# A three-layer decoder block: mended boundaries between batches, and loops written out as straight code

## The chip, the cores and the metric

The kernel runs on one core of one Trainium2 chip. The metric is the device time of one execution in microseconds; lower is better. Before the change it was 4486.38 us in the median of three runs (4477.06, 4486.38 and 4491.97).

## What is computed

The input is `x` (batch B = 4, sequence S = 1024, width D = 512), a context of the same shape, and a mask of 4 × 1024 × 1024. Three layers follow each other, each closed by a residual sum and a layer norm. Both attentions have 16 heads of 32.

```python
# layer 1, "att 0": gated self-attention
aperture, expression = sigmoid(x @ Wa + ba), sigmoid(x @ We + be)
inner, outer = heads(x @ Wi), heads(x @ Wo)
attn = softmax(inner @ outer.T / sqrt(dh)) * aperture[..., :, None] * expression[..., None, :]
attn = attn / (attn.sum(-1) + 1e-8)
x = layernorm(x + rotate_per_head(attn @ heads(x @ Wv)) @ Wout)
# layer 2, "att 1": masked cross-attention
scores = where(mask == 0, -1e9, (x @ Wq.T + bq) @ (ctx @ Wk.T + bk).T / sqrt(dk))
x = layernorm(x + (softmax(scores) @ (ctx @ Wv.T + bv)) @ Wo.T + bo)
# layer 3: 16 experts, weights rw of each token, causal attention of width 64
q, k, v = (sum_e rw_e * (x @ proj[e]) for proj in (q_proj, k_proj, v_proj))
attn = softmax(where(causal, q @ k.T / 8, -inf)) @ v
x = layernorm(x + sum_e (rw_e * attn) @ o_proj[e])
```

## The kernel before, in words

**Attention.** Both attention layers are one program, `attention`. A batch of a layer is worked in eight *pairs* of heads; a pair goes over eight key tiles of 128. TensorE (PE) makes the scores of a tile ("st", L955, and in layer 2 the mask of keys, L958), ScalarE (ACT) takes their exponentials from a PSUM bank (L1159), PE multiplies by V ("pv", L889). Beside that run the row maxima of a later pair: "sm" on PE (L906), the reduction on VectorE (DVE; L1396 in layer 1, L1392 with the mask of queries in layer 2). When 16 maxima of a pair are there, "mneg" puts them into one row: PE L914, ACT L1102, and a DMA from ACT's queue (L1106) into the tile `stack`, from which "st" reads. SyncE (SP) fills the rest of `stack` by DMAs ("stack", L614); `stack` 0 and 1 hold the first two pairs.

Between two batches stands a *boundary*: V of the next batch ("V", eight tiles, L847, evicted by DVE at L1354); the normalisation of the last pair ("norm", seven parts in layer 2: L1417, L1421 and L1427); the output projection of the old batch ("ct", "out": ACT L1083, GpSimd (POOL) L827, PE L847, DVE L1450 to L1460, in layer 2 after POOL has added the bias to the residual, "bo", L820); layer norm ("root", ACT L1166, "ln", DVE L1257); K and Q of the next batch ("K", "Q", L847), where the group 0 of each is split in two parts by ACT (L1056) and DVE (L1307); a transposed copy of the result ("xt", PE L1014, ACT L1172), stored by ACT's queue as two transfers of 1 MB into `x_t` (L1179); the result itself stored by SP as one of 2 MB ("store", L632); and in layer 2 the column means of V ("CS", PE L1000, DVE L1402 to L1408) and 16 tiles of mask converted by DVE ("mask", L1347), of which eight are done in the last pair and eight in the boundary. Then pair 0 of the next batch starts with its first "st".

`section_steps(att, nxt)` writes all of this as one list of steps for the stretch "pairs of layer `att`, then the boundary to a batch of layer `nxt`". Every engine runs down this list and issues the steps that are its own, in the list's order. `with_maxima` interleaves the 16 first "sm" with the projections. PSUM is shared as a ring of two half banks (V, K, Q, out, st, xt, CS) and of two wide ones (sm, mneg), filled in the list's order.

The lists are used as five plans. Each engine runs them as

```python
run(Section(plans[0]))                  # opening, to the first batch
with pe.Fori(0, B - 1) as i:
    run(Section(plans[1], i))           # layer 1 to layer 1, three times
run(Section(plans[2]))                  # layer 1 to layer 2
with pe.Fori(0, B - 1) as i:
    run(Section(plans[3], i))           # layer 2 to layer 2, three times
run(Section(plans[4]))                  # the end of layer 2
```

The branches that close PE's two loops stand at L1020 and L1023. Within a loop a semaphore is waited for at a value that grows with `i`: it stands in a register, which an instruction (`REGISTER_ALU`) computes first. Between such waits `alone(eng)` puts an extra instruction that counts up a semaphore which nobody waits for. So that each pass uses whole rounds of a ring, a pass ends with an extra unit where a count is odd ("wpad", L927, and "xpad", L1016).

**Experts.** `expert_layer` does 32 tiles of 128 tokens with eight banks: "p" (PE L1785 with `w_in_e`, DVE multiplies by the weights, POOL adds), "turn", "score", "pv", "out" (PE L1785 with `w_out_e`) and routing on DVE. `token_slot(g, tile)` is the order of one slot, in which the tiles g−1 and g−2 are finished beside tile g. An opening of two slots, a loop of three passes with eight slots each (PE's branch: L1853) and a closing of eight slots follow each other.

Of the kernel before, what the change touches and what calls it, by code (L numbers as in the profile page):

```python
# [6 lines left out]
P = 128  # L7
# [27 lines left out]
HALF_KINDS = ("Q", "K", "EX", "AP", "V", "CS", "st", "out", "xt", "xpad")  # L35
WIDE_KINDS = ("sm", "mneg", "sel", "RZ", "wpad")
# [77 lines left out]
def mask_places(att):  # L114

    if att == 1:
        return {("K", n // 2): (TT + n, 2) for n in range(0, TT, 2)}
# [6 lines left out]
def section_steps(att, nxt):  # L124
# [67 lines left out]
    if nxt is not None:  # L192
# [3 lines left out]
        if nxt == 1:  # L196
# [4 lines left out]
            ks[len(more) - 1] += [("load", "xq", 0), ("load", "xq", 1), ("mxload", 0), ("mxload", 1)] + store  # L201
# [3 lines left out]
            steps += [("Q", 0, 0)] + xt[:2] + [("Q", 0, 1), ("stack", 0), ("Q", 1, 0), ("Q", 1, 1)] + xt[2:HALF]  # L205
            steps += with_maxima([("Q", g, c) for g in (2, 3) for c in range(NC_)], (4, 3, 3, 3))
            steps += first + [("CS", n) for n in range(4)] + xt[HALF:HALF + 2]
            steps += [("mneg", 0), ("stack", 1)] + xt[HALF + 2:]
        else:
# [3 lines left out]
            ks[len(more) - 1] += store  # L213
            ks[5].append(("stack", 0))
# [5 lines left out]
            steps += first + xt[:HALF] + [("mneg", 0), ("stack", 1)] + xt[HALF:]  # L220
# [14 lines left out]
class Plan:  # L235

    def __init__(self, number, att, nxt, loop, steps):

        self.number, self.att, self.nxt, self.loop, self.steps = number, att, nxt, loop, steps


class Section:

    def __init__(self, plan, i=None):

        self.number, self.att, self.nxt, self.loop, self.steps = plan.number, plan.att, plan.nxt, plan.loop, plan.steps
        self.i = i
        one = lambda b: bass.ds(b, 1)
        self.batch = one(i if plan.loop else B - 1)
        self.next_batch = one(i + 1 if plan.loop else 0)  # L250


class Count:
# [13 lines left out]
    def before(self, sec):  # L267

        return self.after(sec, 0)
# [1945 lines left out]
```

## Time and profile before

| | |
|---|---|
| median of three runs | 4486.38 us (4477.06 to 4491.97) |
| the profiled execution | 4494.6 us, its span 4492.8 us |
| PE busy | 4115.9 us (92%) |
| DVE busy | 2571.8 us (57%) |
| ACT busy | 1714.3 us (38%) |
| POOL busy | 1774.8 us (40%) |
| granted TensorE clock, mean | 0.961 |

The span reaches from the first to the last instruction of the profiled execution, whose own time is 1.8 us more. In the rows below a line of the timeline reads: start in us, busy us, engine, code line, operation, output<-input, shapes, the number of instructions merged in it, and in brackets the idle time before it and what ended that. PEld is the weight load of PE; a name with q (ACTq, PEldq) is the sequencer of the engine.

### The profile page before, as it was taken

The numbers are of one execution on the slowest core, as the hardware profiler recorded it, in microseconds if no ns is written. First come the engines' busy times: TensorE is split into PE (matmuls) and PEld (weight loads), VectorE is DVE, ScalarE is ACT, GpSimd is POOL, SyncE is SP. The second block draws the span as 40 slices with busy tenths as digits, with TensorE's granted clock in tenths as the row PEclk, the third lists the DMA queues.
The fourth block names the chain that finished last, engine by engine and source line by source line (L and its number), as shares of the span: only waits on it lengthen the run. The fifth ranks groups of instructions, "written<-read, shape, count | busy, mean of one in ns | idle before, by whom it ended". The sixth has DMA issues, their size and how long they took to land. (4 is left out here: it accounts for less than half of the span.)

```text
span 4492.8 us, 65435 instructions
## 1 busy us (share of the span) xinstructions
PE 4115.9 (92%) x20596; PEld 2370.4 (53%) x20596; DVE 2571.8 (57%) x4094; ACT 1714.3 (38%) x3120; POOL 1774.8 (40%) x1251
## 2 busy tenths in 40 slices
PE   7999899989999998999799989997998599999998
PEld 5344643554364436444544464446443477777776
DVE  4563466346445646674667466756674556565564
ACT  2554255335524552443244324442444322222222
POOL 0323121312222133675367535753663243444443
PEclk9999899989999999999999989998999799999998
DMA  3321322142123224222422242223220300000000
GB/s 96 76 69 42 104 50 53 51 109 50 50 71 86 56 81 137 65 56 91 119 56 57 90 113 62 52 95 108 66 43 20 139 24 27 30 29 30 29 29 12
DMA packets 136379, 294.73 MB, mean 66 GB/s; under 512 B 19856, under 2 KB 37904, under 8 KB 136016
## 3 DMA queue, kind: packets, MB, share of 16 engines
q1 hardware_dynamic: 125520, 272.93, 22.5%
q10 hardware_dynamic: 10496, 17.31, 1.1%
q8 instruction: 185, 3.03, 0.3%
q14 instruction: 178, 1.46, 0.1%
HBM read 145.74 MB, written 43.25 MB: 42 GB/s over the span
## 5 line engine op out<-in xcount | busy, mean ns | idle before, releaser
L1159 ACT ACTIVATE probs_a<-half_a 128x512 f32<-128x512 f32 x2048 | 1123.8, 595 | 992.5 <-PE half_a L958 464.4
L955 PE MATMUL half_a<-stack_a 97*128 97x512 f32 x2048 | 873.3, 485 | 79.6 <-ACT probs_a L1159 48.4
L1396 DVE TENSOR_REDUCE mx_a<-wide_a 128x1 f32<-128x1024 f32 x512 | 604.5, 1220 | 535.6 <-PE wide_a L906 529.9
L1392 DVE CUSTOM_DVE_ANT_0 wide_a<-wide_a,mask_q_a 128x1024 f32<-128x1024 f32 x512 | 619.8, 1245 | 286.6 <-PE wide_a L906 273.2
L906 PE MATMUL wide_a<-stack_a 96*128 96x512 f32 x2048 | 676.1, 435 | 52.1 <-DVE mx_a L1392 19.8
L955 PEld LDWEIGHTS half_a<-stack_a 97*128 97x128 f32 x2048 | 377.8, 194 | 623.4 <-ACT probs_a L1159 356.1
L795 POOL TENSOR_TENSOR psums_a<-psums_a,probs_a 128x1024 f32<-128x1024 f32 x232 | 557.5, 2423 | 140.0 <-ACT probs_a L1159 115.3
L1785 PE MATMUL work_e<-w_in_e,x_e 128*128 128x512 f32 x2304 | 574.2, 401 | 18.5 <-DVEq L2041 11.2
L889 PE MATMUL acc_a<-probs_a,v_a 128*32 128x512 f32 x4096 | 555.0, 613 | 3.1 <-ACT u_a L1130 3.0
L906 PEld LDWEIGHTS wide_a<-stack_a 96*128 96x128 f32 x2048 | 377.7, 194 | 233.2 <-issue 64.3
L1785 PEld LDWEIGHTS work_e<-w_in_e,x_e 128*128 128x128 f32 x2304 | 430.0, 191 | 120.5 <-issue 20.3
L958 PE MATMUL half_a<-mask_k_a,eye_a 128*128 128x512 fp8e5 x1024 | 407.9, 398 | 0.0
L1753 POOL TENSOR_TENSOR weighted_e<-weighted_e 128x512 f32<-128x512 f32 (+2 forms) x288 | 242.1, 841 | 189.1 <-DVEq L2068 150.6
L889 PE MATMUL acc_a<-probs_a,e_one_a 128*2 128x512 f32 x2048 | 269.9, 599 | 0.0
L759 POOL MEMSET stack_a<- 1x2048 f32 x16 | 28.8, 1799 | 520.0 <-PE half_a L847 519.0
L958 PEld LDWEIGHTS half_a<-mask_k_a,eye_a 128*128 128x128 fp8e5 x1024 | 100.8, 98 | 233.3 <-issue 211.1
L847 PE MATMUL half_a<-stack_a,wkv_a 128*128 128x512 f32 x768 | 190.0, 406 | 34.7 <-DVE first_a L1307 28.5
L847 PE MATMUL half_a<-w_a,ct_a 128*128 128x512 f32 x768 | 187.5, 401 | 25.9 <-POOLq L828 19.8
L847 PE MATMUL half_a<-stack_a,w_a 128*128 128x512 f32 x768 | 204.2, 411 | 3.2 <-DVEq L1325 2.2
L2063 DVE TENSOR_TENSOR weighted_e<-work_e,rw_e 128x512 f32<-128x512 f32 x192 | 132.8, 692 | 111.3 <-PE work_e L1785 65.6
L1785 PE MATMUL work_e<-w_out_e,mixed_t_e 128*128 128x512 f32 x768 | 186.4, 399 | 3.3 <-DVEq L2113 3.3
L847 PEld LDWEIGHTS half_a<-stack_a,wkv_a 128*128 128x128 f32 x768 | 150.7, 197 | 71.6 <-DVE first_a L1307 30.2
(244 smaller groups left out, 4586.7 us busy)
## 6 DMA issues: line engine op xcount, KB each, us to landing
stack_a<-qk_a SPq DMA_DIRECT2D x336, 256.0 KB, 4.9
y_a<-x SPq DMA_DIRECT2D x8, 2048.0 KB, 8.9
x<-y_a SPq DMA_DIRECT2D x8, 2048.0 KB, 8.5
mstage_a<-mask SPq DMA_DIRECT2D x32, 512.0 KB, 4.1
mstage_a<-mask_t SPq DMA_DIRECT2D x32, 512.0 KB, 4.2
stack_a<-first_a SPq DMA_DIRECT2D x48, 256.0 KB, 4.7
stage_a<-x_t SPq DMA_DIRECT2D x20, 512.0 KB, 3.7
x_t<-xts_late_a ACTq DMA_DIRECT2D x10, 1024.0 KB, 8.0
```

What stands on the lines that cost most here:

```text
L795: op = lambda h: pool.tensor_tensor(psums[:, h, :], psums[:, h, :], probs[:, kt % 2 * 2 + h, :], ALU.add)
L847: last = pe.matmul(out, a(k), b(k), start=(k == 0 and n == 0), stop=(k == KT - 1 and n == 2))
L889: last = pe.matmul(out, left, right[:, c * CH:(c + 1) * CH], start=opens or ((kt == 0) and not (masked and part)), stop=closes or ((kt == ...
L906: last = pe.matmul(bank[:, c * CH:(c + 1) * CH], stack[0:3 * DH, SLOT[p], h, t * P:(t + 1) * P], stack[0:3 * DH, SLOT[p], 2 + h, c * CH:(c ...
L955: last = pe.matmul(bank[:, :], stack[0:3 * DH + 1, s, 2 + h, kt * P:(kt + 1) * P], stack[0:3 * DH + 1, s, h, c * CH:(c + 1) * CH], start=T ...
L958: last = pe.matmul(bank[:, :], eye8[:, :], mask_k[:, kt, c * CH:(c + 1) * CH], start=False, stop=True)
L1159: act.activation(probs[:, kt % 2 * 2 + h, c * CH:(c + 1) * CH], bank[:, :], ACT.Exp, scale=SCALE).then_inc(free, 1)
L1392: dve.tensor_tensor_reduce(bank[:, :], bank[:, :], mask_q[:, t, :], 1.0, -3e38, ALU.add, ALU.max, mx[:, p % 3, n:n + 1]).then_inc(free, 1)
L1396: dve.tensor_reduce(mx[:, p % 3, n:n + 1], bank[:, :], AX.X, ALU.max).then_inc(free, 1)
L1753: pool.tensor_tensor(buf[:, 0:n], buf[:, 0:n], buf[:, n:2 * n], ALU.add)
L1785: last = pe.matmul(out, a(k), b(k), start=(k == 0 and n == 0), stop=(k == tiles - 1 and n == 2))
L2063: dve.tensor_tensor(prod.rearrange("p (e d) -> p e d", d=HD), bank[:, :].rearrange("p (e d) -> p e d", d=HD), rw[:, t, (w % 2) * 8:(w % 2) ...
```

## The change

The change has two halves.

**Mended boundaries.** In the list of steps:

- Layer 2 to layer 2: the masks 8 to 14 move from the first four K steps, two at each, to V1 to V7, one at each, and mask 15 goes behind out 0. The parts of the last pair's "norm" stand one at a V tile (before, two at V1, V2 and V3).
- In all boundaries "store" comes behind "stack 0" (before, ahead of it).
- Boundary to layer 2: Q(0,0), Q(0,1), stack 0, store, then xt 0 to 3, then Q of the groups 1, 2 and 3 with all 16 "sm" among them, then xt 4 and 5, mneg 0, stack 1, xt 6 and 7, and one "CS" with all 16 small matmuls in one bank and one eviction. Before, xt 0 and 1 stood between the two Q(0), Q of group 1 ahead of the first "sm", three "sm" behind the last Q, and four "CS" units ahead of xt 4.
- Boundary to layer 1: three xt, then mneg 0, stack 1 and five xt (before, four and four). On ACT's queue the row of mneg 0 so goes out ahead of the first `x_t` store.
- ACT runs a one-element exponential (`warm`) behind the second square root of each boundary, and behind the sine of the opening.

**No loops.** Attention has ten plans, one for each batch of each layer and the two ends, and the experts one list of 32 tiles. Every wait is for a constant. The registers, `alone` and the units "wpad", "xpad" and "pad" are gone.

```diff
 def mask_places(att):
     if att == 1:
-        return {("K", n // 2): (TT + n, 2) for n in range(0, TT, 2)}
+        return {**{("V", n + 1): (TT + n, 1) for n in range(TT - 1)}, ("out", 0): (2 * TT - 1, 1)}
...
         for n in range(1 if att == 0 else 7):
-            tail[(n + 1) // 2 + (1 if att == 0 else 0)].append(("norm", PAIRS - 1, n))
+            tail[n + (1 if att == 0 else 0)].append(("norm", PAIRS - 1, n))
...
-            ks[len(more) - 1] += [("load", "xq", 0), ("load", "xq", 1), ("mxload", 0), ("mxload", 1)] + store
+            ks[len(more) - 1] += [("load", "xq", 0), ("load", "xq", 1), ("mxload", 0), ("mxload", 1)]
             for step in ks[:-2]:
                 steps += step
             steps += [("xs", 0, k) for k in range(KT)] + ks[-2] + ks[-1] + [("xs", 1, k) for k in range(KT)]
-            steps += [("Q", 0, 0)] + xt[:2] + [("Q", 0, 1), ("stack", 0), ("Q", 1, 0), ("Q", 1, 1)] + xt[2:HALF]
-            steps += with_maxima([("Q", g, c) for g in (2, 3) for c in range(NC_)], (4, 3, 3, 3))
-            steps += first + [("CS", n) for n in range(4)] + xt[HALF:HALF + 2]
-            steps += [("mneg", 0), ("stack", 1)] + xt[HALF + 2:]
+            steps += [("Q", 0, 0), ("Q", 0, 1), ("stack", 0)] + store + xt[:HALF]
+            steps += with_maxima([("Q", g, c) for g in (1, 2, 3) for c in range(NC_)], (2, 3, 3, 3, 3, 2))
+            steps += xt[HALF:HALF + 2] + [("mneg", 0), ("stack", 1)] + xt[HALF + 2:] + [("CS",)]
         else:
...
-            ks[len(more) - 1] += store
-            ks[5].append(("stack", 0))
+            ks[5] += [("stack", 0)] + store
...
-            steps += first + xt[:HALF] + [("mneg", 0), ("stack", 1)] + xt[HALF:]
+            steps += xt[:HALF - 1] + [("mneg", 0), ("stack", 1)] + xt[HALF - 1:]
...
-    if att == nxt:
-        for kinds, name in ((WIDE_KINDS, "wpad"), (HALF_KINDS, "xpad")):
-            if sum(s[0] in kinds for s in steps) % 2:
-                steps.append((name,))
...
-    plans = [Plan(number, att, nxt, loop, section_steps(att, nxt)) for number, (att, nxt, loop) in enumerate(
-        ((None, 0, False), (0, 0, True), (0, 1, False), (1, 1, True), (1, None, False)))]
+    layers = (None,) + (0,) * B + (1,) * B + (None,)
+    plans = [Plan(n, att, nxt, (n - 1) % B, section_steps(att, nxt)) for n, (att, nxt) in enumerate(zip(layers, layers[1:]))]
...
-        def alone(eng):
-
-            eng.sem_inc(apart, 1)
...
                     elif step in (("out", HALF), ("root",)):
                         c = int(kind == "root")
...
-                        alone(act)
                         act.activation(sd[:, half], tmp[:, half], ACT.Sqrt).then_inc(sd_ready, 1)
+                        if c:
+                            act.activation(warm[:, :], eye[:, 0:1], ACT.Exp)
...
-            run(Section(plans[0]))
-            with act.Fori(0, B - 1) as i:
-                run(Section(plans[1], i))
...
+            for plan in plans:
+                run(plan)
```

**How the instructions move, at three places.** The first is DVE in the boundary from layer 2 to layer 2, where K is split: `first_a` is the part of K that the next matmuls on `stack_a` wait for, `mask_k_a` a mask tile, `w_a` a weight chunk. Before:

```order
L1304 ISA
L1307 SCALAR_TENSOR_TENSOR first_a<-half_a,bk_a,first_a 128x512
L1340 REGISTER_ALU
L1347 TENSOR_SCALAR mask_k_a<-mstage_a 128x1024 x2
L1332 REGISTER_ALU
L1334 TENSOR_TENSOR w_a<-stage_a,w_a 128x1024
L1340 REGISTER_ALU
L1347 TENSOR_SCALAR mask_k_a<-mstage_a 128x1024 x2
L1332 REGISTER_ALU
L1334 TENSOR_TENSOR w_a<-stage_a,w_a 128x1024
L1340 REGISTER_ALU
L1347 TENSOR_SCALAR mask_k_a<-mstage_a 128x1024 x2
```

and now:

```order
L1196 SCALAR_TENSOR_TENSOR first_a<-half_a,bk_a,first_a 128x512
L1221 TENSOR_TENSOR w_a<-stage_a,w_a 128x1024 x2
L1134 RECIPROCAL rstd_a<-sd_a 128x4
L1136 TENSOR_TENSOR sd_a<-rstd_a 128x4
L1138 TENSOR_TENSOR sd_a<-sd_a,tmp_a 128x4
L1140 TENSOR_SCALAR sd_a<-sd_a 128x4
L1142 TENSOR_TENSOR rstd_a<-rstd_a,sd_a 128x4
L1148 TENSOR_SCALAR y_a<-y_a,mv_a,rstd_a 128x512 x2
L1196 SCALAR_TENSOR_TENSOR first_a<-half_a,bk_a,first_a 128x512
```

The eight mask tiles no longer stand between the two `first_a`. They now stand in the V phase of the same boundary, between the evictions `v_a`:

```order
L1239 TENSOR_TENSOR v_a<-half_a,bv_a 128x512
L1232 TENSOR_SCALAR mask_k_a<-mstage_a 128x1024
L1299 RECIPROCAL u_a<-u_a 128x128
L1239 TENSOR_TENSOR v_a<-half_a,bv_a 128x512
L1232 TENSOR_SCALAR mask_k_a<-mstage_a 128x1024
L1299 RECIPROCAL u_a<-u_a 128x128
L1239 TENSOR_TENSOR v_a<-half_a,bv_a 128x512
```

where before there was an eviction, then two parts of the norm at some tiles and none at others.

The second place is PE at the end of the same boundary, from the last "sm" (`wide_a<-stack_a`) to the first "st" (`half_a<-stack_a`). Before:

```order
L906 MATMUL wide_a<-stack_a 128x512 x2
L997 REGISTER_ALU
L1000 MATMUL half_a<-ones_a,vsum_a 32x1 x4
L943 REGISTER_ALU
L1000 MATMUL half_a<-ones_a,vsum_a 32x1 x8
L943 REGISTER_ALU
L1000 MATMUL half_a<-ones_a,vsum_a 32x1 x4
L1014 MATMUL half_a<-eye_a,y_a 128x128 x4
L943 REGISTER_ALU
L1014 MATMUL half_a<-eye_a,y_a 128x128 x4
L912 REGISTER_ALU
L914 MATMUL wide_a<-neg_eye_a,mm_a 16x128
```

and now:

```order
L837 MATMUL wide_a<-stack_a 128x512 x2
L778 MATMUL half_a<-stack_a,w_a 128x512 x6
L944 MATMUL half_a<-eye_a,y_a 128x128 x8
L845 MATMUL wide_a<-neg_eye_a,mm_a 16x128
L944 MATMUL half_a<-eye_a,y_a 128x128 x8
L930 MATMUL half_a<-ones_a,vsum_a 32x1 x16
L886 MATMUL half_a<-stack_a 128x512
```

A Q unit stands behind the last "sm", the CS matmuls behind everything, and the pad unit and the branch are gone.

The third is ACT at the end of a boundary from layer 1 to layer 1 (`mrow_a` is the row of maxima, `xts_early_a` the first half of the transposed copy). Before:

```order
L1172 ACTIVATE xts_early_a<-half_a 128x4x128 x2
L1177 ISA
L1179 ISA
L1179 DMA x_t<-xts_early_a 128x4x512
L503 REGISTER_ALU
L1102 ACTIVATE mrow_a<-wide_a 16x128
L1104 REGISTER_ALU
L1106 DMA stack_a<-mrow_a 1x16x128
```

and now:

```order
L1070 ACTIVATE xts_early_a<-half_a 128x4x128 x3
L1016 ACTIVATE mrow_a<-wide_a 16x128
L1019 DMA stack_a<-mrow_a 1x16x128
L1070 ACTIVATE xts_early_a<-half_a 128x4x128
L1076 DMA x_t<-xts_early_a 128x4x512
```

The row is copied and sent before the first `x_t` store instead of behind it.

## Rows read from the trace of the kernel before

**Rows 1.** The page: the span, and the DMA queue "instruction" (packets, MB, share).
```profile
span 4492.8 us, 65435 instructions
...
q8 instruction: 185, 3.03, 0.3%
```

**Rows 2.** Windows, two boundaries: from:to, length, busy PE, PEld, DVE, ACT, POOL, then clock.
```profile
418.00:540.00 122.00, 108.28 (x473) 86.12 (x466) 54.05 (x78) 24.67 (x40) 27.54 (x20) 0.94 0.33 96
...
3011.00:3150.00 139.00, 115.63 (x497) 89.12 (x489) 83.56 (x129) 29.15 (x47) 50.40 (x33) 0.89 0.39 114
```

**Rows 3.** Groups by line: busy us, mean ns | idle us before, releaser.
```profile
L1159 ACT ACT_TABLE_LOAD x8 | 10.3, 1283 | 44.0 <-issue 24.3 <-PE half_a L955 17.4 <-PE half_a L958 2.3
```

**Rows 4.** Timeline, mneg 0 to the first "st": in the opening, then after an untaken branch.
```profile
113.05 0.38 PE L914 MATMUL wide_a<-neg_eye_a,mx_a 128*16 128x128 f32 x2
...
117.68 0.51 PE L955 MATMUL half_a<-stack_a 97*128 97x512 f32 x1 [4.25 <-DMA stack_a<-mrow_a]
...
1370.06 0.39 PE L914 MATMUL wide_a<-neg_eye_a,mx_a 128*16 128x128 f32 x2
...
1371.17 0.41 ACTq L1179 DMA_DIRECT2D x_t<-xts_early_a  x1
...
1379.43 1.19 PE L955 MATMUL half_a<-stack_a 97*128 97x512 f32 x2 [3.18 <-DMA stack_a<-mrow_a]
```

**Rows 5.** Timeline, first boundary between batches of layer 1: "store", and the first "sm".
```profile
482.75 0.39 SPq L632 DMA_DIRECT2D x<-y_a  x1
...
493.97 2.08 PE L906 MATMUL wide_a<-stack_a 96*128 96x512 f32 x4 [3.11 <-DMA stack_a<-qk_a]
```

**Rows 6.** Timeline of the last boundary of layer 2 to layer 2, around K and Q.
```profile
3088.50 0.69 DVE L1347 TENSOR_SCALAR mask_k_a<-mstage_a 128x1024 fp8e5<-128x1024 int32 x1 [2.55 <-DMA mstage_a<-mask_t]
...
3089.91 7.84 PE L847 MATMUL half_a<-stack_a,wkv_a 128*128 128x512 f32 x24 [9.06 <-DVE first_a L1307]
...
3104.11 0.66 PE L1014 MATMUL half_a<-eye_a,y_a 128*128 128x128 f32 x4 [2.45 <-DVE first_a L1307]
...
3109.64 4.94 PE L847 MATMUL half_a<-stack_a,w_a 128*128 128x512 f32 x21
...
3116.67 1.21 PE L906 MATMUL wide_a<-stack_a 96*128 96x512 f32 x4 [0.66 <-DMA stack_a<-first_a]
```

**Rows 7.** Instructions of DVE that write `mask_k`: ns least/median/most, first and last start.
```profile
L1347 DVE TENSOR_SCALAR mask_k_a<-mstage_a x32: 679/695/1782, 1697.5 to 3088.5; 128x1024 fp8e5<-128x1024 int32 x32
```

**Rows 8.** PE's branches (ns least/median/most), and the first "st" behind a taken one.
```profile
L1020 PEldq COMPARE_BRANCH  x3: 83/5658/7010, 532.3 to 1375.5; - x3
...
L1023 PEldq COMPARE_BRANCH  x3: 83/4589/4834, 2241.2 to 3147.3; - x3
...
L1853 PEldq COMPARE_BRANCH  x3: 79/4164/4281, 3823.0 to 4281.7; - x3
...
539.57 1.22 PE L955 MATMUL half_a<-stack_a 97*128 97x512 f32 x2 [6.67 <-issue]
```

**Rows 9.** Timeline, row DMAs of layer 1: a batch in the loop, the batch behind it.
```profile
577.70 0.58 ACTq L1106 DMA_DIRECT2D stack_a<-mrow_a  x1
...
724.35 0.51 ACTq L1106 DMA_DIRECT2D stack_a<-mrow_a  x1
...
1417.09 0.54 ACTq L1106 DMA_DIRECT2D stack_a<-mrow_a  x1
...
1562.13 0.53 ACTq L1106 DMA_DIRECT2D stack_a<-mrow_a  x1
```

**Rows 10.** Timeline, "out" of the same tiles: around a taken branch, in the closing.
```profile
4029.43 0.94 PE L1785 MATMUL work_e<-w_out_e,mixed_t_e 128*128 128x512 f32 x3
...
4199.54 0.70 PE L1785 MATMUL work_e<-w_out_e,mixed_t_e 128*128 128x512 f32 x2
...
4258.79 0.94 PE L1785 MATMUL work_e<-w_out_e,mixed_t_e 128*128 128x512 f32 x3
...
4422.35 0.94 PE L1785 MATMUL work_e<-w_out_e,mixed_t_e 128*128 128x512 f32 x3
```

More of the change, by code:

```diff
@@ L281, in __init__ @@
         self.count = Count(plans, lambda plan, s: s[0] in kinds)
-        assert not any(n % size for n, plan in zip(self.count.length, plans) if plan.loop)
     def place(self, sec, step):
-        c, size = self.count, self.size
-        n = c.base[sec.number] + c.at[sec.number][step]
-        return n % size, sec.i * (c.length[sec.number] // size) + n // size if sec.loop else n // size
+        n = self.count.upto(sec, step) - 1
+        return n % self.size, n // self.size
     def opens(self, sec, step):
-        return not sec.loop and self.place(sec, step)[1] == 0
+        return self.place(sec, step)[1] == 0
 WAITING = {}
@@ L313, in attention @@
     loads = kind_count("load")
+    assert not any(len(some) % 2 for some in loads.at)
     pool_splits = Count(plans, lambda plan, s: s[0] == "vsum" or (s[0] == "split" and not fast(plan, s[1])))
@@ L318, in attention @@
     los = Count(plans, two_engine)
-    assert not any(n % 2 for n in loads.length)
     stacks = [Count(plans, lambda plan, s, k=k: s[0] == "stack" and SLOT[s[1]] == k) for k in range(SLOTS)]
@@ L1193, in run @@
                         act.drain().then_inc(turn_sem, 1)
[L1195 to L1201 removed]
+                        act.activation(warm[:, :], eye[:, 0:1], ACT.Exp)
+            for plan in plans:
+                run(plan)
         @block.vector
@@ L1735, in _, with run @@
             pool.sem_inc(stored, 1)
-            def run(sec):
-                for step in sec.steps:
+            def run(steps):
+                for step in steps:
                     kind = step[0]
@@ L1787, in parts, with run @@
                 return last
-            def run(sec):
-                for step in sec.steps:
+            def run(steps):
+                for step in steps:
                     kind = step[0]
@@ L1847, in run @@
                                      lambda k: w_out[:, 0, k, :], lambda k: w_out[:, 1, k, :], FK)
-                    else:
-                        last = pe.matmul(bank[:, 0:P], ones[:, :], eye[:, :], start=True, stop=True)
                     last.then_inc(work_full[b], 1)
-            run(Section(plans[0]))
-            with pe.Fori(0, B - 1) as i:
-                run(Section(plans[1], i))
-            run(Section(plans[2]))
+            run(plan.steps)
         @block.scalar
@@ L1863, in _, with run @@
             act.drain().then_inc(norm_sem, 1)
-            def run(sec):
-                for step in sec.steps:
+            def run(steps):
+                for step in steps:
                     kind = step[0]
@@ L2030, in route, with run @@
                 dve.drain()
-            def run(sec):
-                for step in sec.steps:
+            def run(steps):
+                for step in steps:
                     kind = step[0]
@@ L2138, in run @@
                         dve.drain().then_inc(rstd_ready, 1)
[L2140 to L2143 removed]
+            run(plan.steps)
 def constants():
```

369 lines of the change are left out of this document (91 added, 278 removed).

## The prediction

> **What bounds the kernel now.** I read first the page's busy times: PE works 92% of the span, so only what PE waits for, or what it does at the lower clock, can be won. The page also gives the instruction stream, 65435 instructions in 4492.8 us [rows 1]. Then the windows, to find where PE is idle. Inside the pairs it is nearly full; the idle time stands in the boundaries. In one of layer 1, PE is busy 108.28 of 122.00 us at a granted clock of 0.94, in one of layer 2 115.63 of 139.00 us at 0.89 [rows 2]. PE runs at one of two clocks (1.2 or 2.4 GHz), so a mean of 0.94 over 122 us is 2 × 0.06 × 122 = 14.6 us at half speed, a loss of 7.3 us; in layer 2 it is 30.6 us and a loss of 15.3. Then the timelines of the boundaries, for what ended each wait [rows 4 to 6], and last the branches and the pace of equal stretches with and without registers [rows 8 to 10].
>
> **Table load.** The first exponential of each batch has a table load of 1.28 us ahead of it, eight in all [rows 3]. It starts when the first scores are there, and both half banks stay full until it ends, so PE waits with it. `warm` puts it behind the second square root, where ACT has slack beside the layer norm of DVE. I count all of it: 8 × 1.28 = 10.3 us. If it delays an eviction of K there, part comes back; if all of it did, the term is 0.
>
> **Three boundaries of layer 1.** (a) The 2 MB store is issued at 482.75, ahead of `stack` 0, and the first "sm" waits 3.11 us for that [rows 5]. With `stack` 0 ahead of the store I take all of it, and 1.5 us of the 7.3 that the clock costs there, since the clock falls behind this wait: 4.6 each. Nobody waits for the store before the first exponential of the next batch, so a later store costs nothing. (b) From mneg 0 to the first "st" it is 1379.43 − 1370.06 = 9.37 us, since the row's DMA is issued behind the 1 MB `x_t` store of 1371.17. In the opening, where no such store exists, it is 117.68 − 113.05 = 4.63 us [rows 4]. The difference is 4.7; five xt stand there now instead of four, about 0.7 us more, which I subtract: 4.0 each. The xt units fill PE in the meantime, so they cost nothing until the row lands; the evictions of five on ACT (about 3 us) fit in the 4.6. (c) Behind a taken branch the first "st" comes after 6.67 us of idle time [rows 8], behind the untaken one after 3.18 [rows 4]: 3.5 us more, twice. Sum: 3 × 8.6 + 7 = 32.8 us.
>
> **Boundary from layer 1 to layer 2.** No branch and no masks moved. It takes the new order of Q, xt, stack and store, bounded by 0 and the sum of (a) above and (b) below, 4.6 + 3.8 = 8.4 us; I take 5.
>
> **Three boundaries of layer 2.** (a) K of group 1 waits 9.06 us for DVE's `first_a`, which stands behind masks that themselves wait for their DMA (2.55 us before the last one). The 24 matmuls behind that wait take 7.84 us where the later ones take 4.94/21 × 24 = 5.65: 2.2 us at the lower clock. With the masks out of the K steps both go: 11.3 us [rows 6]. (b) From there to the first "sm" Q and xt alternate: 2.45 us of waiting at 3104.11, then 0.66 before "sm" at 3116.67, with only xt and Q of group 1 as cover. With the two Q(0) back to back `stack` 0 is issued about one eviction and one xt pair earlier. This is between 2.45 us (that wait alone) and 5.8 (both waits, and the four xt at 0.66 each that stood in the chain); I take 3.8, nearer to the waits that a row shows. Four CS units, each waiting for its eviction, become one off the path: 0.6. (c) Seven masks now stand between the evictions of V. DVE's own time for one is 0.70 us in the median but 1.78 at most [rows 7]. V gives DVE a tile in 12 × 4.94/21 = 2.8 us [rows 6], so seven add between 0 (they fit in the gaps) and 7 × 0.70 = 4.9; nearer to the gaps, since "ct" waits for POOL's bias sums anyway: +1.5. (d) The two taken branches cost 4.59 and 4.83 us [rows 8], 9.4 in sum, of which some of the fetch lies beside the wait for the row: 8. Sum: 3 × (11.3 + 3.8 + 0.6 − 1.5) + 8 = 50.6 us.
>
> **Pairs.** Between the same two row DMAs, four pairs apart, a batch in the loop takes 724.35 − 577.70 = 146.65 us, the batch behind it, with constant waits, 1562.13 − 1417.09 = 145.04: 0.40 us a pair [rows 9]. 24 pairs of layer 1 give 9.7 us. For layer 2 I show no such pair of rows; bounds are 0 and 9.7, I take the middle, 4.8. `alone` goes in all 64: 0 to 5, I take 2.5. Sum: 17 us.
>
> **Experts.** Six slots around the last taken branch take 4199.54 − 4029.43 = 170.1 us, the same six in the closing 4422.35 − 4258.79 = 163.6 [rows 10]. Of the 6.5 us the branch is 4.2 [rows 8] and registers the other 2.3, or 0.39 a slot. 24 slots give 9.4, two branches 8.4, pads and `alone` about 3: 21 us.
>
> **The sum** is 10.3 + 32.8 + 5 + 50.6 + 17 + 21 = 136.7 us, against the profiled execution's 4494.6: 4357.9. That execution is 8.2 above the median, 4486.4, so I predict **4350 us**.
>
> **What a taken branch costs.** PE's own record shows it: 7.01 and 5.66 us in layer 1, 4.83 and 4.59 in layer 2, 4.28 and 4.16 in the experts; untaken 0.08 [rows 8]. The Trainium skill ("Advanced Engine Details and Errata", section Control Flow Timing) gives a compare-and-branch as about 108 ns. By that figure six would cost 0.65 us together, the 23.4 us that my sum has for them would be 0.6, and the time 4373. The trace disagrees for taken ones, and decides.
>
> **Rivals.**
>
> *The waits come back elsewhere.* In layer 2, V becomes bound by DVE: eight masks of 0.70 at V are 5.6 us, the first "sm" waits for `stack` as it does in layer 1, 3.1 us, and the clock falls behind that wait, 2.2 us; three times, 32.7. And `warm` only moves its 10.3 us. For it: in the boundary of layer 2 DVE is the second busiest, 83.56 of 139 us [rows 2], and single masks took 1.78 us, over twice the median [rows 7], so something on the chip can slow them. Against it: PE had 23 us of idle time in that window, which is room. The time is 4350 + 43 = 4393. The Trainium skill ("SBUF — State Buffer", section Who interferes with whom) says that VectorE and GpSimd share one pair of ports under an exclusive lock. No row here shows the lock itself, and the sentence before goes by the masks' times alone. Chance 0.20.
>
> *Only the loops count.* The boundaries are bound by work that I take for cover, and the new order gives nothing: what is left is the branches (23.4), pairs (17) and experts without their branches (12.6), 53 us: 4433. For it: the boundary's matmuls are the same. Against it: waits of 9.06 and 3.11 us with nothing else that PE could do. Chance 0.07.
>
> *The clock stays up.* The half-speed losses of six boundaries are 3 × 7.3 + 3 × 15.3 = 68 us [rows 2], of which my sum has only 11. If shorter waits keep PE at the full clock for some 60% of the rest, 34 us come on top, and 10 more if the pairs of layer 2 and `alone` reach their upper bounds: 4306. Chance 0.14.
>
> *Straight code stalls.* Here the kernel gets slower. The code of three passes now stands in memory three times, PE alone has nearly twice as many instructions, and each must be brought in once. Its place is every block of code that arrives late; its price is what a taken branch costs, which is such an arrival with nothing fetched ahead: 4.2 us at least [rows 8]. 33 of these eat the 137 us; from 36 on the kernel is slower by over 0.3%, and with 60 it stands at 4486 − 137 + 250 = 4600. Against it: a loop's passes are fetched again each time, so the 3.03 MB of the instruction queue [rows 1] hardly change, and the stretches without a loop run faster than those within, not slower [rows 9, 10]. Chance 0.02. The Trainium skill ("Runtime: NRT & Kernel Launch", section Instruction fetch mechanics) says that a taken branch outside the window forces a fetch while straight code is fetched ahead, its cost mostly hidden. The trace agrees with both halves.
>
> **Chances and range.** My forecast has 0.57, the rivals 0.20, 0.07, 0.14 and 0.02. A measurement of this kernel can tell about 0.3%, 13 us, from no change. Four of the five cases, 0.98, lie further below than that; 0.02 of these I move to "the same", for faults that no case names, so faster 0.96, same 0.02, slower 0.02. The range reaches from just under the clock case to 12 us above the case of the waits that come back: 4300 to 4405. Above it lie the two last-named bad cases (0.09) and little else; below it the better half of the clock case. The unknown terms alone (0 to 10.3 for the table, 0 to 7.8, three times 0 to 4.9, 0 to 9.7, 0 to 5) move the forecast by less than 30 us either way.
>
> **What would show it.** In the changed profile: no table load between the first "st" and the first exponential; from mneg 0 to the first "st" about 5 us in layer 1, where 9.4 stood; no wait of PE for `first_a` above 1 us in K of layer 2, and a clock of 0.92 or more in that window; no wait of the first "sm" above 1 us; a boundary from the last "pv" to the first of some 118 us in layer 1 and 133 in layer 2; expert slots of equal length in all four batches. I am wrong if V of layer 2 spreads by over 5 us, if "sm" waits 3 us for `stack`, or if PE has gaps of 4 us and more with nothing to release them, away from any boundary.

## The result and the profile after

The changed kernel takes 4324.1 us (4323.7 to 4327.5, four runs), the kernel before beside it 4483.1: a ratio of 0.9644, 95% interval 0.9632 to 0.9655. That is 159 us or 3.6% faster. I had forecast 4350 and a range of 4300 to 4405; the gain is 22 us larger than the forecast's 137. But the experiments show that its two halves are not the ones I had summed up. In the two profiled executions, from which the rows and the table by stage come, the difference is 4492.8 − 4322.0 = 170.8 us, since the one of the kernel before lies above its median.

The page of the changed kernel, as [rows 1]:

```profile
span 4322.0 us, 56842 instructions
...
q8 instruction: 165, 2.70, 0.3%
q14 instruction: 112, 0.92, 0.1%
```

8,600 instructions fewer are executed, and fewer packets of code are fetched than before, though the program is longer: 165 + 112 packets, where the page before has 185 [rows 1] and, on its second queue,

```profile
q14 instruction: 178, 1.46, 0.1%
```

The windows of the same two boundaries as [rows 2], now from the last "pv" to the first of the next batch (after the clock stand the mean share of the DMA engines that was busy, and GB/s):

```profile
409.50:521.30 111.80, 108.45 (x482) 85.54 (x474) 55.54 (x80) 29.37 (x49) 26.03 (x18) 0.99 0.34 98
2893.00:3026.00 133.00, 115.01 (x514) 88.26 (x506) 88.69 (x127) 33.77 (x56) 51.58 (x33) 0.94 0.43 129
```

The windows of [rows 2] leave out the last 8 and 10 us of their boundaries. The whole ones before:

```profile
418.10:548.20 130.10, 113.98 (x484) 89.20 (x476) 55.61 (x80) 29.49 (x48) 32.75 (x22) 0.91 0.32 92
3011.40:3159.80 148.40, 123.25 (x512) 93.00 (x505) 85.52 (x132) 34.28 (x55) 50.52 (x33) 0.87 0.43 122
```

In layer 1 PE idled 16.1 of 130.1 us at a granted clock of 0.91, and now idles 3.4 of 111.8 at 0.99; in layer 2 it idled 25.2 of 148.4 at 0.87, and now 18.0 of 133.0 at 0.94.

Table loads by line, as [rows 3]: L1062 is the square root, which had its eight loads before as well, and L1064 is `warm`. No exponential of attention has one any more.

```profile
L1062 ACT ACT_TABLE_LOAD x8 | 10.3, 1283 | 0.1
L1064 ACT ACT_TABLE_LOAD x8 | 10.3, 1283 | 0.1
```

Timeline, end of the first boundary of layer 1, as [rows 4], and its stack 0 and store, as [rows 5]:

```profile
510.21 0.39 PE L845 MATMUL wide_a<-neg_eye_a,mx_a 128*16 128x128 f32 x2
...
511.17 0.53 ACTq L1019 DMA_DIRECT2D stack_a<-mrow_a  x1
...
512.45 0.59 ACTq L1076 DMA_DIRECT2D x_t<-xts_early_a  x1
...
515.32 0.76 PE L886 MATMUL half_a<-stack_a 97*128 97x512 f32 x2 [0.43 <-DMA stack_a<-mrow_a]
...
474.90 5.92 SPq L582 DMA_DIRECT2D stack_a<-qk_a  x6
...
480.87 1.27 SPq L597 DMA_DIRECT2D x<-y_a  x1
```

The row goes out ahead of the `x_t` store, and the first "st" starts 5.1 us after mneg 0, where it was 9.37. PE waits 0.43 us there. The store (480.87) comes behind stack 0 (474.90).

Timeline of K, Q and the first "sm" in the last boundary of layer 2, as [rows 6]:

```profile
2950.16 19.41 PE L778 MATMUL half_a<-stack_a,wkv_a 128*128 128x512 f32 x84 [0.34 <-DVE y_a L1329]
...
2978.76 1.09 PE L944 MATMUL half_a<-eye_a,y_a 128*128 128x128 f32 x8 [1.19 <-DVE first_a L1196]
...
2985.24 1.19 PE L837 MATMUL wide_a<-stack_a 96*128 96x512 f32 x2 [4.47 <-DMA stack_a<-first_a]
```

K runs through without the wait of 9.06 us, but the first "sm" now waits 4.47 us for `stack` 0, where it waited 0.66.

The conversions of the mask, as [rows 7], now beside V:

```profile
L1232 DVE TENSOR_SCALAR mask_k_a<-mstage_a x32: 681/1055/2287, 1629.2 to 2925.1; 128x1024 fp8e5<-128x1024 int32 x32
```

Their median rose from 0.70 to 1.06 us and the longest from 1.78 to 2.29. In both kernels those that ran while POOL did nothing took 0.69 us, and those above 0.75 us all ran beside an instruction of POOL; in V that is above all the bias sum of "bo". V itself did not become longer by it: its 96 matmuls take 22.1 us in these boundaries before and after.

Pace of four pairs, as [rows 9], and of six expert slots, as [rows 10]:

```profile
549.38 0.53 ACTq L1019 DMA_DIRECT2D stack_a<-mrow_a  x1
...
693.93 0.53 ACTq L1019 DMA_DIRECT2D stack_a<-mrow_a  x1
```

```profile
3876.39 0.70 PE L1621 MATMUL work_e<-w_out_e,mixed_t_e 128*128 128x512 f32 x2
...
4036.69 0.70 PE L1621 MATMUL work_e<-w_out_e,mixed_t_e 128*128 128x512 f32 x2
```

144.55 us, where 146.65 (loop) and 145.04 (behind it) stood, and 160.3 us, where 170.1 and 163.6 stood. So both are shorter than the stretches that already had constant waits.

A table by stage, from the starts of the first and last "pv" of each batch and of the first and last unit "out" of the experts (us in the profiled executions; the last three columns are experiments told below):

| stage | before | after | e1_straight_old | e2_alone | p1_cs_early |
|---|---|---|---|---|---|
| opening | 126.1 | 122.2 | 123.9 | 124.1 | 122.5 |
| pairs of layer 1, four batches | 1158.6 | 1143.8 | 1143.2 | 1152.3 | 1145.3 |
| three boundaries of layer 1 | 386.6 | 337.6 | 366.0 | 339.9 | 336.1 |
| boundary 1 to 2 | 138.4 | 132.5 | 130.8 | 136.7 | 127.5 |
| pairs of layer 2 | 1194.9 | 1188.9 | 1181.3 | 1196.7 | 1181.3 |
| three boundaries of layer 2 | 452.0 | 398.4 | 417.6 | 412.5 | 385.8 |
| to the first expert "out" | 145.2 | 142.3 | 142.3 | 147.6 | 143.7 |
| experts | 875.0 | 839.9 | 839.5 | 863.7 | 839.9 |
| rest | 15.9 | 16.5 | 16.7 | 15.9 | 16.6 |

Four fifths of the 170.8 us come from three places: 49 us in boundaries of layer 1, 54 in those of layer 2, 35 in the experts.

### The profile page after: what moved, and what is told of

It reads as the page before. It is cut to its first block and busy times, and to the rows that moved or that the text cites. A ratio compares the mean times of both kernels' runs of the same rounds, so it can differ in the third digit from the quotient of the medians.

```text
span 4322.0 us, 56842 instructions
## 1 busy us (share of the span) xinstructions
PE 4054.9 (94%) x20584; PEld 2348.4 (54%) x20584; DVE 2600.2 (60%) x4082; ACT 1718.5 (40%) x3131; POOL 1788.5 (41%) x1251
## 5 line engine op out<-in xcount | busy, mean ns | idle before, releaser
L886 PE MATMUL half_a<-stack_a 97*128 97x512 f32 x2048 | 862.8, 480 | 42.9 <-ACT probs_a L1056 24.0
L837 PE MATMUL wide_a<-stack_a 96*128 96x512 f32 x2048 | 671.1, 432 | 44.1 <-DMA stack_a<-first_a 18.1
L778 PE MATMUL half_a<-stack_a,wkv_a 128*128 128x512 f32 x768 | 179.4, 391 | 6.5 <-DVE y_a L1329 5.2
L778 PEld LDWEIGHTS half_a<-w_a,ct_a 128*128 128x128 f32 x768 | 146.9, 193 | 67.7 <-issue 21.8
```

The costliest lines, as they stand in the source:

```text
L778: last = pe.matmul(out, a(k), b(k), start=(k == 0 and n == 0), stop=(k == KT - 1 and n == 2))
L837: last = pe.matmul(bank[:, c * CH:(c + 1) * CH], stack[0:3 * DH, SLOT[p], h, t * P:(t + 1) * P], stack[0:3 * DH, SLOT[p], 2 + h, c * CH:(c ...
L886: last = pe.matmul(bank[:, :], stack[0:3 * DH + 1, s, 2 + h, kt * P:(kt + 1) * P], stack[0:3 * DH + 1, s, h, c * CH:(c + 1) * CH], start=T ...
```

## The experiments

Each run is compared with the kernel before on the same chip; the median of before lay between 4483 and 4489 in these comparisons. Differences against the changed kernel are therefore taken from the ratios (0.001 is 4.5 us); each ratio is uncertain by 0.0012 to 0.0020, which makes a difference of two uncertain by 8 to 10 us. A stage of the table rests on one execution of each kernel.

### Which half does it: e1_straight_old

Straight code with constant waits, every boundary as before.

```diff
-            steps += [("Q", 0, 0), ("Q", 0, 1), ("stack", 0)] + store + xt[:HALF]
+            steps += [("Q", 0, 0)] + xt[:2] + [("Q", 0, 1), ("stack", 0), ("Q", 1, 0), ("Q", 1, 1)] + xt[2:HALF]
...
-            steps += xt[:HALF - 1] + [("mneg", 0), ("stack", 1)] + xt[HALF - 1:]
+            steps += first + xt[:HALF] + [("mneg", 0), ("stack", 1)] + xt[HALF:]
```

and so on for all lines of `section_steps` and `mask_places`, CS and `warm`.

> The changed kernel without loops, registers, alone and pads, but with every boundary as before (masks in K, store ahead of stack 0, xt and Q in the old order, four CS, no warm). Against 4483 before and 4324 after. Theory 1 (the two halves add up, each about as large as my terms say, experts and pairs larger): branches 23, pairs 21, experts without branches 27: 4412 (4400 to 4425), experts as short as in the changed kernel. Theory 2 (the loops carry nearly all, boundaries were mostly longer for the registers in them): 4350 to 4370. Theory 3 (boundaries carry nearly all): 4440 or more.

Measured: 4362.6 us, ratio 0.9721 (0.9708 to 0.9735). 125 us of the 160 come with the loops alone, 35 with the boundaries. That is theory 2, whose 4350 to 4370 it hits; my own sum had 53 for the loops (branches 23.4, pairs 17, experts without branches 12.6) and 84 for the boundaries and the table load. The windows of the same two boundaries:

```profile
411.40:533.40 122.00, 111.42 (x482) 87.36 (x474) 55.58 (x80) 29.25 (x48) 30.54 (x22) 0.95 0.32 96
2929.40:3067.80 138.40, 116.35 (x514) 88.32 (x507) 88.17 (x132) 34.14 (x55) 50.64 (x33) 0.93 0.44 131
```

By the table, a boundary of layer 1 falls from 129 to 122 us without its order being touched, one of layer 2 from 151 to 139. In the profiled executions the loops are worth 131.5 us: 63 in the seven boundaries, 29 in the pairs, 35.5 in the experts, the rest at the ends.

### What in the loops: e2_alone, e9_alone_pe, e10_alone_act

```diff
+        def alone(eng):
+            eng.sem_inc(apart, 1)
```

called again where it was called before: e2 on all engines, e9 on PE, e10 on ACT.

> The changed kernel with alone(eng) back at all of its 100-odd places in the code. My sum gives alone 5.5 us in all: 4330. Rival: the experts won 35 us where I forecast 21, and the 14 more are the extra instructions between waits, on ACT and PE at every unit of a bank: 4340 to 4350, with the experts 14 us longer than in the changed kernel and the pairs within 5 us.

> The changed kernel with alone back on PE only (5 places in the code). With all of them the kernel took 65 us more. Theory 1 (the extra instruction delays the engine that is the bound, so PE's own are half of it or more): 4356 or more. Theory 2 (it lengthens the chains by which PE gets its banks back, so they sit on ACT and DVE): 4335 or less here.

> The changed kernel with alone back on ACT only (36 places in the code). Theory 1 (PE's own count): 4324 to 4335. Theory 2 (chains over ACT: in the run with all of them PE waited 9.7 and 9.6 us more in the experts for ACT's steps behind turn and prob_t): 4344 to 4365.

Measured: e2 4389.3, ratio 0.9778 (0.9765 to 0.9792), so 60 us for an instruction that does nothing, more than either expectation had. e9 4323.4, ratio 0.9639 (0.9619 to 0.9658): no difference. e10 4347.2, ratio 0.9689 (0.9671 to 0.9706): 20 us. If the parts add, the rest, some 40 us, is on DVE, POOL and SP together; it was not split further. How many there are and how long each lasts (ns least/median/most), of attention (L474) and experts (L1597) in e2:

```profile
L474 DVEq EVENT_SEMAPHORE  x940: 21/21/21, 16.3 to 3406.6; - x188
L474 ACTq EVENT_SEMAPHORE  x729: 17/17/38, 13.8 to 3414.3; - x183
...
L1597 DVEq EVENT_SEMAPHORE  x560: 21/21/50, 3445.0 to 4383.6; - x187
L1597 PEldq EVENT_SEMAPHORE  x537: 51/51/51, 3475.2 to 4370.1; - x179
L1597 ACTq EVENT_SEMAPHORE  x430: 17/17/17, 3436.6 to 4383.2; - x144
```

PE has 541 of 51 ns and pays nothing that a measurement can tell. But not every `alone` is one instruction more: the pages of the changed kernel, e2, e9 and e10 begin

```profile
span 4322.0 us, 56842 instructions
span 4389.5 us, 60013 instructions
span 4323.9 us, 57093 instructions
span 4340.6 us, 57602 instructions
```

All 4,444 of e2 add 3,171 instructions, PE's 541 add 251 and ACT's 1159 add 760; the others stand where the changed kernel has some other semaphore instruction. 251 of 51 ns are 12.8 us of PE's sequencer, and 760 of 17 ns are 12.9 us of ACT's. The first cost nothing, the second 20 us (10 to 30 with the uncertainty), so the length alone doesn't give the price. That ACT's come between PE and a bank that it waits for is the reading that theory 2 had, and its total came true; its place did not: only 4 of e10's 18.6 us in span lie in the experts, 7 in the pairs of layer 1, and the rest in small parts. Of e2's 67.5 us more in span, the experts have 24, the layer-2 boundaries 14, the pairs 16. What PE waits for in the experts of e2, in the list of waits (total us, times, longest); where the changed kernel has one wait each, of 4.7 and of 3.7 us, e2 has 13 and 16, and e10 only 10 (8.4 us) and 1 (5.2 us):

```profile
PE work_e L1741 <- ACTq L1825: 9.7, 13, 5.8
PE work_e L1747 <- ACTq L1835: 9.6, 16, 4.8
```

and in the kernel before:

```profile
PE work_e L1820 <- ACTq L1913: 18.9, 25, 6.0
```

By subtraction, the loops' 125 us are 60 for `alone`, some 23 for six taken branches as priced in the prediction, and about 40 for registers and padding units. The last part was not tried by itself, since a loop needs its registers. The branches' price can be compared in layer 1: before, the two boundaries that end in a taken one last 130.1 us each and the third 126.4, so 3.7 us a branch, where the prediction had 3.5; in e1 all three last 122.0, so 4.4 us of each are something else.

Much of this came as time in which PE did the same work faster. Its busy time is 4115.9 us on the page before (20596 matmuls), 4066.1 on e1's and 4054.9 on the changed kernel's (20584 each). The mean granted clock was 0.961, 0.972 and 0.975. So 50 of e1's 131.5 us in span, and 61 of the changed kernel's 170.8, are shorter matmuls (their ends are modelled in the profile, so this is an estimate), and the rest is idle time.

### The boundaries, part by part

Four runs undo one part of the change each. e3 puts the store ahead of stack 0 in boundaries to either layer; these are its lines for layer 1:

```diff
-            ks[5] += [("stack", 0)] + store
+            ks[len(more) - 1] += store
+            ks[5].append(("stack", 0))
```

> The changed kernel with store ahead of stack 0 again, in all boundaries. My sum: 4.6 us in each of three boundaries of layer 1 (3.1 of waiting, 1.5 of clock), 14 us: 4338, with a wait of about 3 us of the first sm for stack_a<-qk_a. Rival: in straight code the first sm comes later after stack 0 than it did and hides the store: 4324 within 4 us.

Measured: 4341.8, ratio 0.9679 (0.9665 to 0.9693), 16 us. The boundaries of layer 1 take 12.3 us more by the same table, 4.1 each (my term: 4.6), and the wait is there in the list of waits:

```profile
PE wide_a L838 <- DMA stack_a<-qk_a: 8.1, 3, 2.8
```

```diff
                         if c:
-                            act.activation(warm[:, :], eye[:, 0:1], ACT.Exp)
```

> The changed kernel without the one-element exponential. My sum: 8 x 1.28 = 10.3 us: 4334. Rival: the load before the first exponential is covered by the second scores and sm, and the loads only change places: 4324 within 4 us.

Measured: 4336.4, ratio 0.9666 (0.9652 to 0.9679), 10 us, where 10.3 were expected, though the uncertainty would allow 2 to 18.

```diff
-            steps += xt[:HALF - 1] + [("mneg", 0), ("stack", 1)] + xt[HALF - 1:]
+            steps += first + xt[:HALF] + [("mneg", 0), ("stack", 1)] + xt[HALF:]
```

> The changed kernel with four xt ahead of mneg 0 in boundaries to layer 1, so that the row is sent behind the 1 MB x_t store. My sum: 4.0 us in each of three boundaries: 4336, with about 9 us from mneg 0 to the first st. Rival: without registers on ACT the store and the row follow each other faster and half of it is gone: 4330.

Measured: 4344.4, ratio 0.9685 (0.9671 to 0.9699), 18 us; 5.4 for each boundary of layer 1 by the table's stages (my term: 4.0). The waits of "st" for the row, in this run and then in the changed kernel:

```profile
PE half_a L886 <- DMA stack_a<-mrow_a: 22.1, 7, 6.1
```

```profile
PE half_a L886 <- DMA stack_a<-mrow_a: 8.2, 7, 4.3
```

13.9 us for three boundaries is 4.6 each. The rest may be the clock, 0.95 in each of the three where the changed kernel has 0.97 to 0.99.

```diff
-        return {**{("V", n + 1): (TT + n, 1) for n in range(TT - 1)}, ("out", 0): (2 * TT - 1, 1)}
+        return {("K", n // 2): (TT + n, 2) for n in range(0, TT, 2)}
...
-            tail[n + (1 if att == 0 else 0)].append(("norm", PAIRS - 1, n))
+            tail[(n + 1) // 2 + (1 if att == 0 else 0)].append(("norm", PAIRS - 1, n))
```

> The changed kernel with the masks 8 to 15 back in the first four K steps of layer 2 and the last pair's norm parts in pairs again. My sum: 3 x (11.3 - 1.5) = 29 us back: 4353, a wait of PE for first_a of about 9 us in each of the three boundaries. Rival: the masks only move their cost from K to V, where PE now waits for VectorE's y_a and POOL's ct: 4324 to 4335.

Measured: 4344.5, ratio 0.9688 (0.9675 to 0.9701), 20 us, between the two. The wait in K is back at full size, so it was real and not moved:

```profile
PE half_a L778 <- DVE first_a L1196: 26.1, 4, 9.5
```

In its three boundaries the run loses 22.6 us (421.0 against 398.4), 7.5 each where I had 9.8 net. From the first K to the first Q it takes 12 us more, as I had it (11.3). From the first V to the first K it takes 49.1 to 49.4 us, and the changed kernel 50.6, 53.6 and 52.8: the moved masks cost 3.1 us a boundary there, not the 1.5 of my sum. Only 0.9 us of that comes before the first "out"; the rest is in "out", behind whose first tile mask 15 now stands, which took 1.27, 2.28 and 2.29 us in the three. PE's waits for `y_a` are 13.2 us in the changed kernel and 8.8 in this run.

### The order that cost time: e7_old_q, p1_cs_early, p2_q_first

```diff
-            steps += [("Q", 0, 0), ("Q", 0, 1), ("stack", 0)] + store + xt[:HALF]
-            steps += with_maxima([("Q", g, c) for g in (1, 2, 3) for c in range(NC_)], (2, 3, 3, 3, 3, 2))
-            steps += xt[HALF:HALF + 2] + [("mneg", 0), ("stack", 1)] + xt[HALF + 2:] + [("CS",)]
+            steps += [("Q", 0, 0)] + xt[:2] + [("Q", 0, 1), ("stack", 0)] + store + [("Q", 1, 0), ("Q", 1, 1)] + xt[2:HALF]
+            steps += with_maxima([("Q", g, c) for g in (2, 3) for c in range(NC_)], (4, 3, 3, 3))
+            steps += first + [("CS", n) for n in range(4)] + xt[HALF:HALF + 2]
+            steps += [("mneg", 0), ("stack", 1)] + xt[HALF + 2:]
```

> The changed kernel with the old order of Q, xt, sm, CS in boundaries to layer 2 (store stays behind stack 0). My sum: 3.8 + 0.6 in four boundaries: 4342. Rival: the new order only trades waits, since the first sm of layer 2 now waits 4.5 us for stack 0 in each of the four boundaries, where it waited 0.7: 4324 within 4 us.

Measured: 4304.1, ratio 0.9587 (0.9573 to 0.9600): the old order is 26 us faster than the new one. Neither expectation holds; this part of the change is a loss, and the changed kernel is fast in spite of it. (The profiled execution of e7 is the slowest of its five, 4315.6, so the stages are read from p1.) First, the new order has the wait of the first "sm". The list of waits of the changed kernel, then of the kernel before:

```profile
PE wide_a L837 <- DMA stack_a<-first_a: 18.1, 4, 4.5
```

```profile
PE wide_a L906 <- DMA stack_a<-first_a: 3.0, 4, 1.0
```

15 us more, since before, two units of Q of group 1 covered the transfer. Second, pair 0 is slower in three of the four batches of layer 2. Two proposals were to tell whether that is the late CS.

p1 is e7 with the one CS unit of the change, placed behind Q of group 1; p2 is the new order with one Q and CS between the store and xt 0:

```diff
+            steps += [("Q", 0, 0), ("Q", 0, 1), ("stack", 0)] + store + [("Q", 1, 0), ("CS",)] + xt[:HALF]
+            steps += with_maxima([("Q", 1, 1)] + [("Q", g, c) for g in (2, 3) for c in range(NC_)], (3, 3, 3, 3, 4))
+            steps += xt[HALF:HALF + 2] + [("mneg", 0), ("stack", 1)] + xt[HALF + 2:]
```

> A proposal: the changed kernel with the old order of Q, xt and sm in boundaries to layer 2 (the run with it took 4304.1), but the single CS unit of the change, and that ahead of xt 2, where VectorE idles before the first sm. If four CS units with their evictions cost what the trace shows (9.9 us of PE waiting for vmean in four boundaries) and the new place is free: 4294. If CS was hidden by the wait for mneg 0: 4304 within 4 us. If its 3.4 us on VectorE delay the first sm: 4310.

> A second proposal: the order of the change with one Q of group 1 and CS between stack 0 and xt 0, and the 16 sm spread over the five Q left. The wait of the first sm for stack_a<-first_a falls from 4.5 to 1.7 us in four boundaries (11 us) and the slow first pair behind the late CS goes (3.6 us in each of four, 14 us): 4299. If the slow first pair has another cause than CS: 4313.

Measured: p1 4302.2, ratio 0.9591 (0.9572 to 0.9610), the same as e7 within the intervals, so four CS units cost no more than one that could be told, the second of its three expectations (4304); p2 4308.2, ratio 0.9600 (0.9582 to 0.9618), nearer to its second expectation, another cause than CS. Both are faster than the changed kernel by 20 to 24 us, and p2's waits for `stack` 0 have fallen from 18.1 to 6.1 us. p2's pairs of layer 2 stay long (1192.8 us in its profile, p1's 1181.3), and PE waits up to 2.1 us for `probs` in pair 0 again, so the late CS is not what slows pair 0. The timeline of the changed kernel shows what does, from the end of its last boundary:

```profile
3011.91 3.72 POOL L705 MEMSET stack_a<- 1x2048 f32 x2 [50.14 <-PE half_a L778]
...
3018.40 0.77 PE L886 MATMUL half_a<-stack_a 97*128 97x512 f32 x1 [2.06 <-issue]
...
3043.88 2.02 POOL L734 COPY psums_a<-probs_a 128x1024 f32<-128x1024 f32 x2 [0.31 <-issue]
...
3046.07 1.09 ACT L1056 ACTIVATE probs_a<-half_a 128x512 f32<-128x512 f32 x2 [3.58 <-POOLq L742]
...
3046.72 0.51 PE L886 MATMUL half_a<-stack_a 97*128 97x512 f32 x1 [1.79 <-ACT probs_a L1056]
```

and the same chain in p1:

```profile
2986.49 3.72 POOL L705 MEMSET stack_a<- 1x2048 f32 x2 [44.32 <-PE half_a L778]
...
2996.25 0.76 PE L886 MATMUL half_a<-stack_a 97*128 97x512 f32 x1 [2.00 <-issue]
...
3017.27 2.02 POOL L734 COPY psums_a<-probs_a 128x1024 f32<-128x1024 f32 x2 [0.31 <-issue]
```

POOL's work for the next batch (the memset of `stack`, the split of group 1, the weights, then the first sums of pair 0) may start when the last Q is done. In the new order "sm" units stand between the Q to the very end, so the memset starts 6.5 us ahead of the first "st"; in the old, three "sm" come behind the last Q and it starts 9.8 ahead. The first sum then comes 25.5 us after the first "st" instead of 21.0, ACT waits 3.58 us for POOL before it may write over `probs`, PE waits 1.79 for ACT, and the granted clock of pair 0 is 0.94 where p1 has 1.00, in windows of 31 us from its first "pv":

```profile
3026.20:3057.20 31.00, 29.21 (x145) 13.67 (x144) 19.04 (x31) 12.13 (x22) 19.45 (x11) 0.94 0.30 75
```

```profile
3003.60:3034.60 31.00, 30.88 (x163) 14.61 (x163) 20.32 (x33) 13.91 (x26) 23.01 (x12) 1.00 0.21 56
```

PE gets through 163 matmuls in the one and 145 in the other. No run moves POOL's work alone, but the batches and runs differ in the lead of the memset over the first "st", and the wait goes with it: 6.4 to 6.8 us of lead and waits of 0.7 to 2.1 us in thirteen batches of the changed kernel, e3, e5 and p2; 7.7 to 8.1 us and at most 0.2 in one batch each of the changed kernel, e3 and e5; 9.8 to 14.2 us and at most 0.3 in all batches of the old order (before, e1, e7, p1). p1's boundaries of layer 2 are also 4.2 us shorter each than the change's. The version to keep is the old order of Q, xt and "sm" with the rest of the change.

### Do the halves add: e8_new_in_loops

The kernel before with loops, registers, `alone` and pads, and all boundaries of the change with `warm`.

> The kernel before, loops, registers, alone and pads kept, with all the boundaries of the change and warm. Without loops the boundaries gave 38 us (4362.6 to 4324.1). Theory 1 (the halves add): 4488 - 38 = 4450. Theory 2 (boundaries hold waits that registers and alone lengthen, so mending them wins more here): my first sum for the boundaries, 75 us: 4413. Theory 3 (the new boundaries have more register waits on the path, and win less): 4465 or more.

Measured: 4434.6, ratio 0.9884 (0.9868 to 0.9899), so 52 us, against 35 in straight code. It lies between theories 1 and 2 (whose 75 us should have been 84, as above, so 4404): mending the boundaries gives more where loops are kept. So the halves overlap: 52 alone and 125 alone would be 177, and both together give 160. The 17 us are uncertain by about 11. By stage they lie in the boundaries of layer 2: there the mending gives 38.3 us with loops (452.0 to 413.7) and 19.2 without (417.6 to 398.4), while in layer 1 it gives 28.4 either way (386.6 to 358.2, 366.0 to 337.6). What in these boundaries makes the difference stays open.

## Why the prediction was right, and where it was not

**The total** was right, 137 us forecast and 159 measured, by two errors that nearly cancel: the loops gave 72 us more than forecast, the boundaries 49 less. That it fell within 22 us is luck in this respect. The prediction's rows gave the sizes of single waits well, and its split into halves badly.

**Loops: forecast 53 us, measured 125.** Most of the missing time is in the boundaries. There I had counted branches alone (7 and 8 us, nothing for the boundary between the layers), with no term for registers, `alone` and padding units. e1 shows 20.6, 34.4 and 7.6 us in their spans: 48 more than the 15, of which `alone` accounts for 2.3, 14 and 4 in e2. "Pairs" and "Experts" are the second place: the stretches with constant waits behind the loops were taken as what straight code would give, and `alone` was priced at 2.5 us in the pairs and, with the pads, about 3 in the experts. But those stretches held `alone` too. e1 gives 29 us in the pairs (17 forecast) and 35.5 in the experts (21 forecast), and e2 puts 16 and 24 down to `alone`. A rule by which it costs its own time on the engine that is the bound is what e9 speaks against: on PE it cost nothing that can be told, on ACT 20 us. The 0.40 us a pair and the 0.39 a slot are what rows 9 and 10 show; no run has registers without `alone`, so they were not tried.

**Taken branches.** No run has a loop without `alone` and registers, so their share stays mainly as it was read from the records; the 3.7 us by which the boundaries of layer 1 differ before agree with the term of 3.5. In e8 the taken branches lasted up to 6.9 us in layer 1, up to 7.0 before.

**Layer 1: forecast 8.6 us for each boundary and 1.28 for the table.** Straight code with old boundaries takes 366.0 us in three, the change 337.6: 9.5 each, where these two terms make 9.9. e3 gives 4.1 for the store (4.6), e6 5.4 for the row (4.0), e4 10 us for the table over the whole kernel (10.3). These terms hold within the uncertainty, and they were read from waits with one cause each.

**Layer 2: forecast 14.2 us for each boundary, and 1.28 for the table; measured 6.4** (417.6 − 398.4 over three), and 7.6 us lost in the pairs behind them. (a) and (c), the masks: 9.8 net expected, 7.5 measured; (a) was right, and (c) was 3.1 where I had 1.5, for the most part in "out". (b), the order of Q, xt and stack: +3.8 expected, and the sign was wrong. I had counted which waits would vanish and not what covered `stack`'s transfer (two units of Q), and had not asked when POOL's chain for the next batch could start. My own rival named the wait for `stack` in layer 2, at 3.1 us; it is 4.5. The prediction had even named an "sm" that waits 3 us for `stack` as a sign of being wrong, and it came. So that rival was true in part, and the larger gain from the loops hid it. Its other parts did not come: V stays at 22.1 us, and `warm` gave its 10. The boundary between the layers, forecast to win 5 us, takes 1.7 more than in e1 (132.5 against 130.8).

**The clock.** This is the other way to see the same miss. My sum had 11 us for the clock (1.5 and 2.2 in each of three boundaries) and 126 for waits, branches and instructions. Of the 170.8 us in span, 61 are shorter matmuls, as the clock's rise from 0.961 to 0.975 would give (0.014 × 4322 = 61 us), and 110 are idle time. 50 of the 61 come with the loops already. By the prediction's own conversion, length times what the clock lacks to 1, the six boundaries lost 88 us before, and 30 now; it had worked from windows that leave out the last 8 to 10 us, and so had 68. So the rival "the clock stays up", to which I gave 0.14, was true in its mechanism and beyond its size, and the time did not fall to its 4306 because less idle time went than I had summed (and its 10 us for the pairs and `alone` should have been 7.4, 4309 in all). That the higher clock follows from fewer waits is the reading of all these rows; no run changes the one without the other.

**Straight code stalls:** no sign. Fewer packets of code were fetched, and away from the boundaries PE has no gap above 1.7 us that nothing releases. The wait that is new in the pairs, up to 1.79 us in pair 0 of layer 2, has a releaser and goes with the order of Q.

## What to carry to other kernels

Price an instruction that only a sequencer runs by the engine it is on, not by its length: 13 us of them on PE cost nothing here, 13 us on ACT cost 20, and a few ns times thousands is a per cent. When a stretch is taken as the model of a changed program, list what it still shares with the old one. When a unit moves, ask what its own time was covering, and which slow engine's chain starts behind the unit that now comes last. And look at the busy time of the bound engine as well as at its waits: where its clock depends on them, removing waits can give back as much again in shorter instructions.

## What the runs showed of the hardware that was not expected

An instruction that only counts up a semaphore lasts 51 ns on PE's sequencer, 17 on ACT's and 21 on DVE's (median in e2), and 4,444 of them, 3,171 more instructions than without, cost 60 us of 4324.

In two batches of the changed kernel a wait of 1.79 us in pair 0 came with a granted clock of 0.94 over the 31 us around it, where the run without the wait had 1.00: 0.06 × 31 = 1.9 us, as much again as the wait. In a third batch a wait of 1.26 us left the clock at 1.00.

A conversion of a mask tile by VectorE took 0.69 us while GpSimd did nothing and up to 2.29 us beside its work, and an eviction of V by the same engine, beside the same work, at most 0.693 us.
